# The ninth spherical number of each edge: copied over 128 lanes by a DMA instead of spread by a fifth selector product

## The reference, cut to what matters

```
def tensor_product(x_e, sh, w, C):            # x_e [E,64], sh [E,9], C [64,9,128]
    acc = sh[:, 0:1] * (x_e @ C[:, 0, :])
    for s in range(1, 9):
        acc = acc + sh[:, s:s + 1] * (x_e @ C[:, s, :])
    return acc * w
k = tensor_product(x_dst, edge_sh, wk, Cqk);  v = tensor_product(x_dst, edge_sh, wv, Cv)
```

## Time and profile before

| | |
|---|---|
| median of 3 runs | 2818.77 us (2813.94 to 2825.93) |
| profiled execution | 2815.99 us, span 2814.2 us |
| busy, share of the span | PE 85%, DVE 89%, POOL 68%, ACT 53% |
| mean granted TensorE clock | 0.914 of full |
| DMA | 399 MB, mean 142 GB/s |

### The profile page before, as it was taken

The page is one execution under the profiler, slowest core; times in us unless marked ns, Lnnn a source line. Parts: engine busy times, 40 slices in busy tenths (PEclk is TensorE's granted clock), DMA queues, the critical chain, the costliest instruction groups (busy, mean ns, idle before and its releaser), DMA issues.

```text
span 2814.2 us, 46735 instructions
## 1 busy us (share of the span) xinstructions
PE 2384.4 (85%) x12225; PEld 1707.2 (61%) x12225; DVE 2512.5 (89%) x3400; ACT 1481.3 (53%) x2844; POOL 1923.7 (68%) x1744
## 2 busy tenths in 40 slices
PE   2112599999999999999999999999999999999624
PEld 2001266776677767777677767777677777777511
DVE  7676378999999999999999999999999999999737
ACT  2101255666566556666566666666566666666410
POOL 2562277777777777777777777777777777777040
PEclk7555589999999999999999999999999999999855
DMA  9985222444444444554445454444444445555440
GB/s 254 251 206 131 67 73 82 126 148 142 145 141 145 144 141 147 148 149 149 141 145 149 145 145 148 146 148 147 141 144 148 145 146 149 147 147 145 127 127 12
DMA packets 228907, 399.41 MB, mean 142 GB/s; under 512 B 62577, under 2 KB 93221, under 8 KB 228104
## 3 DMA queue, kind: packets, MB, share of 16 engines
q1 hardware_dynamic: 165910, 277.42, 31.6%
q0 software_dynamic: 53904, 110.47, 16.0%
q10 hardware_dynamic: 8794, 8.14, 0.9%
HBM read 312.90 MB, written 82.94 MB: 141 GB/s over the span
## 4 chain that ended last, share of the span: by engine, by line
PE 37%; DVE 17%; issue 8%; DMA 2%; DVEq 1%; ACT 0%; SPq 0%; POOL 0%; ACTq 0%
PE bank L1178 7%; PE bank L1179 6%; PE bank L1180 6%; DVE xa_t L1671 4%; PE bank L1206 3%; PE bank L1195 3%; DVE x_r L1746 2%; DVE z_l L1679 2%; PE bank L1260 2%; DVE val L1704 2%; PE bank L1185 2%; PE bank L1184 2%; PE bank L1228 1%; DVE val L1741 1%; DVE qt L1694 1%
## 5 line engine op out<-in xcount | busy, mean ns | idle before, releaser
L788 POOL DMA_INDIRECT gathered<-xtab_d,src_g x784 | 872.4, 1113 | 300.8 <-issue 209.9
L788 POOL DMA_INDIRECT gathered<-qtab_d,dst_g x784 | 861.7, 1099 | 254.5 <-issue 241.9
L1178 PE MATMUL bank<-z_h,wt_h 128*128 128x512 f32 x1568 | 730.4, 466 | 15.1 <-DVE val L1704 14.8
L930 ACT ACTIVATE z_h<-xa_t 128x512 fp32r<-128x512 f32 x980 | 603.7, 630 | 189.4 <-DVE xa_t L1671 174.2
L1671 DVE TENSOR_TENSOR xa_t<-bank,r_r 128x512 f32<-128x512 f32 x980 | 654.9, 686 | 15.3 <-PE bank L1206 9.1
L1180 PE MATMUL bank<-z_h,wt_l 128*128 128x512 f32 x1568 | 620.3, 396 | 0.0
L1179 PE MATMUL bank<-z_l,wt_h 128*128 128x512 f32 x1568 | 619.5, 395 | 0.0
L1679 DVE TENSOR_TENSOR z_l<-xa_t,z_h 128x1024 fp32r<-128x1024 f32 x392 | 475.7, 1214 | 27.3 <-ACT z_h L930 27.3
L1178 PEld LDWEIGHTS bank<-z_h,wt_h 128*128 128x128 f32 x1568 | 300.7, 192 | 117.7 <-issue 47.7
L1206 PE MATMUL bank<-s,sel 128*128 128x512 bf16 x980 | 349.3, 389 | 11.5 <-issue 7.1
L1180 PEld LDWEIGHTS bank<-z_h,wt_l 128*128 128x128 f32 x1568 | 294.3, 188 | 71.9
(11 more groups left out here) (248 smaller groups left out, 4095.1 us busy)
## 6 DMA issues: line engine op xcount, KB each, us to landing
nrow_d<-x_r SPq DMA_DIRECT2D x196, 288.0 KB
ea<-in_ea_t SPq DMA_DIRECT2D x392, 128.0 KB
exb<-exd_d SPq DMA_DIRECT2D x196, 256.0 KB
dmb<-exd_d SPq DMA_DIRECT2D x196, 256.0 KB
ea_c<-in_ea_t SPq DMA_DIRECT2D x56, 448.0 KB
gathered<-xtab_d,src_g POOLq DMA_INDIRECT x784
gathered<-qtab_d,dst_g POOLq DMA_INDIRECT x784
keep_c<-keep_d SPq DMA_DIRECT2D x56, 112.0 KB
```

The costliest lines, as they stand in the source:

```text
L788: rows_in = pool.indirect_dma_start(rows[:, c % 4, k, :], None, table, bass.IndirectOffsetOnAxis(ap=picked[:, s, at:at + 1], axis=0))
L930: act.activation(z_h[:, c % 2, i, :], z[:, i, :], ACT.Copy).then_inc(zh_ok, 1)
L1178: pe.matmul(ps[:, :], wt_h[rows, w, :], high, start=start, stop=False)
```

## The change

The fifth selector product of each group is taken out, and with it its wait and its turn of the two banks (the banks now go by `i % 2`). In its place SP issues one DMA a group that reads the row of spherical number 8 for the 512 edges (2 KB) and writes it to all 128 lanes of a new tile `s8`, two groups deep, in a part of `x_r` that is free during the loop. The fifth outer product reads `s8` instead of the bank. The number then comes as plain float32 instead of as the sum of three bf16 parts. Two semaphores of the beginning are merged with others to make room for those of the new load.

```
+        s8 = x_flat[:, 2 * G + 8 * RW:4 * G + 8 * RW].rearrange("p (b g) -> p b g", b=2)
...
-                past(sp, shb_ps, j, c, 4, NJ)
+                past(sp, shb_ps, j, c, 4, NS)
...
+            def load_last_harmonic(j, c):
+                if isinstance(j, int) and c == 0:
+                    sp.wait_ge(qtab_out, 16)
+                past(sp, z_ok, j, c, 2, NJ)
+                hold()
+                sp.dma_start(s8[:, c % 2, :], harmonics_t[S - 1:S, bass.ds(group(j, c) * G, G)].to_broadcast([P, G])
+                             ).then_inc(s8_in[c % 2], 16)
...
+                if live(j, c + 2):
+                    load_last_harmonic(j, c + 2)
...
-                if not isinstance(j, int) or c * NJ + i >= 2:
+                if i >= 2:
                     done(pe, z_ok, j, c, NJ, i - 1 - NJ)
-                pe.matmul(bank[2 + (NJ * c + i) % 2][:, :], sel[:, i, :], s3[:, c % 4, :], start=True, stop=True
+                elif not isinstance(j, int) or c >= 1:
+                    done(pe, z_ok, j, c - 1, NJ, i - 2)
+                pe.matmul(bank[2 + i % 2][:, :], sel[:, i, :], s3[:, c % 4, :], start=True, stop=True
...
-                    if i + 2 < NJ and live(j, c + 1):
+                    if i + 2 < NS and live(j, c + 1):
...
-                done(dve, shb_ps, j, c, NJ, i + 1 - NJ)
+                if i < NS:
+                    done(dve, shb_ps, j, c, NS, i + 1 - NS)
+                else:
+                    landed(dve, s8_in, j, c)
...
-                dve.tensor_tensor(z[:, i, :], bank[2 + (NJ * c + i) % 2][:, :], xt[:, c % 2, :], ALU.mult
+                dve.tensor_tensor(z[:, i, :], bank[2 + i % 2][:, :] if i < NS else s8[:, c % 2, :], xt[:, c % 2, :], ALU.mult
```

More of the change, by code:

```diff
@@ L27 @@
 NJ = 5
+NS = NJ - 1
 CK, CV, W1KV = 0, NJ, 2 * NJ
@@ L316, in gnn_two_layers @@
         sh_in = sem("sh_in")
-        x_in = sem("x_in")
         flags_done = sem("flags_done")
@@ L322, in gnn_two_layers @@
         split_out = sem("split_out")
-        sel_done = sem("sel_done")
         padded = sem("padded")
@@ L367, in gnn_two_layers @@
         s3_in = [sem(f"s3_in{i}") for i in range(2)]
+        s8_in = [sem(f"s8_in{i}") for i in range(2)]
         rs_in = [sem(f"rs_in{i}") for i in range(2)]
@@ L570, in loads_and_stores @@
             sp.dma_start(shf, harmonics_t.rearrange("s (c w) -> (s c) w", c=SC)).then_inc(sh_in, 16)
-            sp.dma_start(x_r[:, :, 0:D], a["x"].rearrange("(t p) d -> p t d", p=P)).then_inc(x_in, 16)
+            sp.dma_start(x_r[:, :, 0:D], a["x"].rearrange("(t p) d -> p t d", p=P)).then_inc(flags_out, 16)
             sp.wait_ge(flags_done, 2)
@@ L588, in loads_and_stores @@
             sp.dma_start(mid_b[:, :], sums_d[EH // 2 - 2:EH // 2 - 1, :].to_broadcast([P, D])).then_inc(mid_in, 16)
-            sp.wait_ge(flags_out, 48)
+            sp.wait_ge(flags_out, 64)
             sp.wait_ge(x1_ok, 1)
@@ L835, in _ @@
             act.wait_ge(padded, 1)
-            act.activation(sel[0:SP3, :, :].rearrange("k j m -> k (j m)"), sel_f[:, :], ACT.Copy).then_inc(sel_done, 1)
+            act.activation(sel[0:SP3, :, :].rearrange("k j m -> k (j m)"), sel_f[:, :], ACT.Copy).then_inc(head_ok, 1)
             act.activation(wt_h[:, :, :], wt[:, :, :], ACT.Copy).then_inc(wth_ok, 1)
-            act.wait_ge(head_ok, 1)
+            act.wait_ge(head_ok, 2)
             act.activation(head_sel[:, BP - H:BP], headones[:, bass.ds(0, H, DH)], ACT.Copy).then_inc(head_ok, 1)
@@ L1142, in _ @@
             pe.wait_ge(q_ok, len(NODE_BLOCKS))
-            pe.wait_ge(sel_done, 1)
             pe.wait_ge(wtl_ok, 4)
-            pe.wait_ge(head_ok, 2)
+            pe.wait_ge(head_ok, 3)
             pe.wait_ge(padded, 2)
@@ L1605, in _ @@
                               ).then_inc(quad_step, 1)
-            dve.wait_ge(x_in, 16)
+            dve.wait_ge(flags_out, 64)
             dve.wait_ge(quad_step, 15)
```

## The result

The changed kernel takes 2838.20 us (median of 6 runs, 2835.28 to 2848.43) against 2816.36 us (6 runs, 2812.54 to 2825.93): a ratio of 1.0068, with a 95% interval of 1.0048 to 1.0089. It is slower: by 21.8 us between the medians, and by 14 to 25 us by the interval. The profiled execution has a span of 2833.4 us, 19.2 more than the one of before.

A forecast was written before the change was run, and what follows sets the result against it. PE was taken to pace plain steps, DVE just behind, POOL a third engine near the bound. +16 for POOL, +4 early, -3 for PE and DVE made +17 on 2815.99 us: 2833, or 2836 as median; range 2803 to 2865.

The forecast's parts named there:

- What bounds: Loop: PE paces plain steps at 11.21 us, DVE 0.1 us behind; POOL paces the first seven cycles at 82.12 us.
- The selector product, 46 us at most, some 9 where DVE takes over: PE: 196 dropped products save 46 us if PE alone counted; DVE takes over after 0.08 us a plain step, leaving 9.
- -3: Loop: the gain of PE and DVE counts only where they set the pace, a third of the loop: -3 us.
- The new load at no cost: SP and DMA: issuing takes 0.66 us and queues nobody; data is used 17 us later, so 0 cost.
- DVE's fifth outer product, 0: DVE: two SBUF inputs take 0.68 against 0.69 us, at most 2 us in all; taken as 0.
- POOL falls back to its pace in two thirds of 20 cycles, +16, less 3: After 1045.97 us: POOL's slower pace, 24 us if in all 20 cycles, two thirds taken: +16; PE and DVE gain 3.
- +4 in the first seven cycles: Start of loop: the first seven cycles, POOL-paced anyway, get 0.6 us longer each, 4 us.
- The walk through a plain step: POOL's gathers beside DVE in a plain step: delays of 0.50 and 0.72 us, caught within the step, cost 0.
- two thirds between holding and losing: 20 cycles after 1045.97 us: POOL keeps its lead in some, falls back in others; two thirds of 24 us taken, 16.
- 9 us faster: Whole kernel: if `tensor_tensor` leaves descriptor generation alone, the sum would be -9 us only.

The follow-up runs named there:

- only POOL is relieved: Kernel before, with GpSimd's copies of row numbers made once before the loop instead of per batch: 2805.99 us, ratio 0.9956.
- the second profile: Kernel before run once more, unchanged, for another profile: 2813.53 us.
- load and bank: Changed kernel with its load every group, but the fifth outer product reads the fourth's PSUM bank again: 2809.83 us, ratio 0.9958.
- the square: Changed kernel and three variants: fifth outer product reads SBUF tile or PSUM bank, load every group or twice only: tile 2838.20, 2846.03 us; bank 2809.83, 2807.92 us.

## Why the prediction was right

The forecast of 2836 us, +17 on the profiled execution, met 2838.20, and its range held it; the profiled execution grew by 19.2. The cause is the forecast one: long gathers, a late query turn, longer cycles behind the eighth scan. How near the number came is partly luck, as the terms show.

- *What bounds:* right for PE and DVE, within 0.1 us in a plain step, and for POOL as a third bound at the start of the loop. The kernel before gains 0.4% when only POOL is relieved, and gains it there: its seven cycles fall to 567.6 us (from 578.9 and 574.1), while the stretch behind the eighth scan stays at 1603.2. Wrong is that POOL paces all seven cycles and is freed by the jump: in the second profile only the first two are longer.
- *The selector product, 46 us at most, some 9 where DVE takes over:* right in kind. A plain step fell from 11.21 to 11.12, forecast 11.13, and PE then waits. A cycle that nothing holds up fell from 80.37 to 80.02 (load and bank), and the stretch behind the eighth scan by 6.1 us (1604.0 to 1597.9), so the gain is had there nearly in full and not by a third, as the sum had it with -3. With the bank as operand and no load, leaving the product out gave 0.46% (13 us); against the kernel with the load alone (2810.70 us) it gave 1 to 3 us. Both are far from 46, and the size between them is not settled.
- *The new load at no cost:* right. 0.35 us on SP (median), no wait of DVE for it in any step, and no more than 2 us in the square's kernels that read the bank.
- *DVE's fifth outer product, 0:* right; with two SBUF operands its median is 684 ns, and the mean over all five with a bank was 686 before.
- *POOL falls back to its pace in two thirds of 20 cycles, +16, less 3:* right in place and cause, near in size by luck. The stretch behind the eighth scan grew by 15.6 us against 13 forecast, and the waits of the query turn that name the cause are there. But it is +21.7 for the operand (1619.6 against 1597.9) less 6.1 for the selector product, so both terms were too small and the errors partly cancel. Nor did cycles fall back to one pace: they take 80.0 to 84.1, and the 1.75 us a cycle from which the 16 was made was one execution's mean.
- *+4 in the first seven cycles:* not shown. It measured -1.3 against one profile of before and +3.5 against the other.
- *The walk through a plain step:* the step where my reasoning was too mild. It took each gather as held by one DVE instruction at most, with 0.50 and 0.72 us as the delays, caught in the same step. In the trace a gather can be held through two or three instructions in a row, 2.2 us more than a free one. The rule behind it was also too broad at the other end: in the kernel before, 380 gathers begin inside L1679, and 174 of them take 0.94 us all the same, 169 of which begin in its last 0.11 us. That the sum came out all the same rests on the choice of two thirds between holding and losing, which was no measurement; with five selector products the same operand cost 59 us of loop, 26 of them through a wait that the changed kernel lacks.

The Trainium skill ("SBUF — State Buffer", section "Who interferes with whom") told the direction, that a DVE instruction with two SBUF inputs contends with a GpSimd instruction that reads SBUF, and the square agrees (28 and 38 us). Its inference that `tensor_tensor` leaves descriptor generation alone, by which the result had been 9 us faster, does not carry over to the indirect DMAs here, for which GpSimd reads row numbers in SBUF: the lengthened gathers are beside `tensor_tensor` and scan instructions.

## What to carry to other kernels

When a DVE operand moves from PSUM to SBUF, look at what GpSimd issues beside it, not only at DVE's own duration: the same 0.69 us instruction cost 1% of this kernel through the gathers that it held. Look also at its neighbours in DVE's order, since two such instructions back to back close the opening in which a gather could get through, and moving two instructions by a few places gave it all back. And to test whether an engine that looks idle for a third of the time is the bound, take unrelated work off it, and off the kernel before as a control: here that gave 37 us with the suspected stalls still in place, and 13 in the control. Last, profile the kernel before twice: a pace read from one execution was the weakest number of this forecast.

## What was not expected of the hardware

A gather that begins inside a DVE instruction with two SBUF inputs is not always let go at that instruction's end. Of the gathers that begin inside the fifth outer product of the changed kernel, 72 took 1.4 to 1.5 us, so were let go at its end, and 15 took 2.5 to 2.6, so were held through L1694 as well; nine more began at the start of the instruction ahead of it, L1724, and took 3.1 to 3.2. What separates the 72 from the 15 was not found: both kinds begin within 0.15 us of its start. Nor is every gather that begins inside such an instruction held at all: in the changed kernel 355 begin inside L1694, and 239 of them begin in its last 0.11 us and take the 0.94 us of a free one; none of those that take longer begins in its last 0.2 us.
